# An attention and two feed-forward layers on one core: the order of the engines' work within a pair of tiles, and in the last steps, written anew

## What is computed

```python
h = shift_token(x)                      # second half of the columns moved down by one row
q, k, v = split(h @ wqkv)               # 8 heads of 64
q, k = rotary_xpos(l2norm(q) * qs, l2norm(k) * ks)
o = local_attention(q, k, v)            # windows of 128: each row sees its own and the previous window
x = x + o @ wo
h = layernorm(shift_token(x)) * g + b
a, g = split(h @ w1 + b1)               # 2 x 682 columns
x = x + (a * gelu(g)) @ w2 + b2
```

## Time and profile before

| | |
|---|---|
| median of three runs | 2774.15 us (2766.67 to 2779.47) |
| the profiled execution | 2765.1 us |
| its span, first to last instruction | 2762.9 us |
| granted TensorE clock, mean | 0.983 |
| instructions | 65920 |
| second phase | from about 291 us to the end |

### The profile page before, as it was taken

How to read it: one execution, slowest core, us unless ns; L and a number is a source line. 1 busy time by engine, 2 the same in 40 slices (tenths; PEclk the granted TensorE clock), 3 DMA queues, 4 the chain that set the end, 5 groups by cost and what they waited for, 6 DMA issues and landing times.

```text
span 2762.9 us, 65920 instructions
## 1 busy us (share of the span) xinstructions
PE 2674.0 (97%) x22240; PEld 2347.6 (85%) x22240; DVE 2257.7 (82%) x7122; ACT 1889.5 (68%) x4798; POOL 1649.6 (60%) x1753
## 2 busy tenths in 40 slices
PE   8998699999999999999999999999999999999996
PEld 5776478888888888888988888888888888888886
DVE  5776578888888888888887888888888888988884
ACT  5565367767777777777776777767777767777773
POOL 3444456666656566655555666676666666666662
PEclk9999799999999999999999999999999999999998
DMA  5566210000000000000002311110111110011110
GB/s 181 182 198 196 101 44 28 24 28 25 24 26 28 26 26 28 21 26 28 26 26 81 107 35 32 36 36 27 32 35 32 36 35 29 30 35 32 36 30 22
DMA packets 144511, 140.39 MB, mean 51 GB/s; under 512 B 16024, under 2 KB 126128, under 8 KB 143408
## 3 DMA queue, kind: packets, MB, share of 16 engines
q1 hardware_dynamic: 144176, 136.18, 15.6%
HBM read 80.02 MB, written 51.92 MB: 48 GB/s over the span
## 4 chain that ended last, share of the span: by engine, by line
PE 83%; DVE 2%; DMA 1%; ACT 1%; issue 1%; SPq 1%; POOL 0%; DVEq 0%; POOLq 0%; ACTq 0%
PE p_wide L95 13%; PE p_wide L97 12%; PE p_wide L96 12%; PE p_values L1680 9%; PE p_turn L1668 8%; PE p_mixed L95 5%; PE p_mixed L97 5%; PE p_mixed L96 5%; PE p_score L95 4%; PE p_turn L1635 2%; PE p_score L96 2%; PE p_score L97 2%; PE p_turn L1642 2%; PE p_mixed L1600 1%; PE p_mixed L1698 1%
## 5 line engine op out<-in xcount | busy, mean ns | idle before, releaser
L1114 POOL TENSOR_TENSOR prob<-prob,rinv 128x512 f32<-128x512 f32 (+1 forms) x512 | 498.4, 989 | 504.6 <-DVE rinv L1402 504.2
L1217 ACT ACTIVATE prob<-prob,least 128x256 f32<-128x256 f32 (+1 forms) x1024 | 498.5, 488 | 68.4 <-DVE least L1394 65.4
L1394 DVE CUSTOM_DVE_ANT_0 prob<-p_score,mask,inv_norm 128x256 f32<-128x256 f32 (+1 forms) x1024 | 442.1, 459 | 53.3 <-issue 50.0
L1092 POOL TENSOR_TENSOR inv_norm<-norm_clipped,minus_half 128x8 f32<-128x8 f32 x256 | 439.0, 1715 | 74.2 <-DVE norm_clipped L1360 67.4
L1226 ACT ACTIVATE pT<-p_turn 128x512 f32<-128x512 f32 (+1 forms) x512 | 270.4, 566 | 245.5 <-PE p_turn L1668 243.8
L95 PE MATMUL p_wide<-hT_h,w_h 128*128 128x256 f32 (+1 forms) x1408 | 414.1, 294 | 5.3 <-DVE hT_l L1450 4.2
L97 PE MATMUL p_wide<-hT_h,w_l 128*128 128x256 f32 (+1 forms) x1408 | 396.5, 282 | 0.0
L96 PE MATMUL p_wide<-hT_l,w_h 128*128 128x256 f32 (+1 forms) x1408 | 395.8, 281 | 0.0
L95 PE MATMUL p_wide<-wqkv_h,xT_h 128*128 128x512 f32 x768 | 330.0, 430 | 6.2 <-DVE rope_sin L1344 4.0
L1248 ACT ACTIVATE gelu<-p_wide,columns 128x256 f32<-128x256 f32 x320 | 151.7, 474 | 228.5 <-PE p_wide L97 226.9
L97 PE MATMUL p_wide<-wqkv_h,xT_l 128*128 128x512 f32 x768 | 307.2, 400 | 0.0
(11 more groups left out here) (134 smaller groups left out, 7620.7 us busy)
## 6 DMA issues: line engine op xcount, KB each, us to landing
x_tile<-x_rows SPq DMA_DIRECT2D x192, 128.0 KB, 2.1
a_wraw<-in_w_all SPq DMA_DIRECT2D x32, 264.0 KB, 4.4
w_high<-a_wraw_h SPq DMA_DIRECT2D x32, 264.0 KB, 2.4
w_low<-a_wraw_l SPq DMA_DIRECT2D x32, 264.0 KB, 3.0
a_x<-in_x SPq DMA_DIRECT2D x32, 256.0 KB, 4.7
x_rows<-a_x SPq DMA_DIRECT2D x64, 128.0 KB, 1.8
x_tile<-x_rows SPq DMA_DIRECT2D x128, 64.0 KB, 2.0
mid_rows<-x_mid SPq DMA_DIRECT2D x128, 64.0 KB, 1.5
```

Source lines behind the costliest of these rows:

```text
L1092: pool.tensor_tensor(r[:, t.slot(2), heads], rt[:, heads], half[:, heads], ALU.pow).then_inc(pool_r[n], 1)
L1114: pool.tensor_tensor(p, p, rinv[:, 2 * m:2 * m + 2].unsqueeze(2).to_broadcast([P, 2, cols.stop - cols.start]), ALU.mult).then_inc(pool_p, 1)
L1217: act.activation(prob[:, h, cols], prob[:, h, cols], ACT.Exp, bias=least[:, h:h + 1], scale=-1.0, accum_out=rsum[:, h:h + 1]).then_inc(act ...
L1394: dve.tensor_tensor_reduce(prob[:, h, cols], p_score[h % 2][:, c0 + cols.start:c0 + cols.stop], mask[:, a.slot(2), cols], r[:, a.slot(2), ...
```

## The change

```diff
@@ PE, first part of step @@
             def step(st_):
                 T, Q = st_.tile, st_.pair
                 T, Q = st_.tile, st_.pair
+                if T(6):
+                    after((act_pT, T(6), 4, 2))
+                    after((pool_p, T(6), 4, 4))
+                turn_probs(T(6), 3)
+                if T(4):
+                    after((dve_kr, T(4), 1, 1))
+                project_v(T(4))
                 if T(5):
-                    vacant((act_pT, T(6), 4, 4), (act_pT, T(6), 4, 2), (dve_kT, T(5), 1, 1), (act_pT, T(7), 4, 4), (dve_kT, T(6), 1, 1), (act_pT, T(7), 4, 2))
-                turn_probs(T(5), 1)
+                    after((act_pT, T(6), 4, 3))
+                    after((pool_p, T(5), 4, 1))
+                turn_probs(T(5), 0)
+                if T(3):
+                    after((dve_x, T(9), 1, 1), (dve_xT, T(4), 1, 1))
+                    if not T(9):
+                        after((dve_xT, T(4), 1, 1))
+                turn_x(T(3))
+                scores(T(5), 1)
+                values(T(6), 0)
+                values(T(6), 1)
...
@@ PE, end of step @@
+                if T(3):
+                    if not T(4):
+                        after((dve_qT, T(3), 1, 1))
+                scores(T(3), 0)
+                if T(2):
+                    after((dve_gt, Q(4), HF + 1, 6), (dve_xT, T(2), 1, 1))
+                project_k(T(2), 0)
+                project_k(T(2), 1)
+                if T(8):
+                    after((dve_gT, Q(4), HF + 1, 6), (dve_xT, T(2), 1, 1))
+                narrow(T(8))
...
@@ DVE, least_of and middle @@
                         need(dve, pe_pT, a.done(4, 2 * group - 2))
-                        at = 2 * a.slot(2) + group
-                        dve.memset(took[:, at:at + 1], 0.0)
...
-                    need(dve, pool_res, c.done(1, -1))
+                    if c.g < LAYER + 2:
+                        need(dve, pool_res, c.done(1, -1))
+                    else:
+                        dve.wait_ge(pool_r1, c.done(1, -1 - LAYER))
...
@@ SP, step, the new order @@
+                refill("q", T(2))
+                store_mid(T(6))
+                load_shifted(T(6))
+                load_x1(T(8))
+                store_mid(T(5))
+                load_shifted(T(5))
+                refill_tables(T(2), 0)
+                refill("w2", T(8))
+                load_x(T(1))
+                refill_tables(T(2), 1)
+                refill("w1", T(6))
                 refill("wo", T(4))
+                load_x1(T(7))
+                store_x(T(8))
+                store_x(T(7))
+                refill("k", T(0))
+                load_x(T(0))
                 refill("v", T(0))
...
@@ ACT, step, the new order from widen's results to the exponentials @@
                 gelu(Q(4), 3)
+                q_high(T(3))
+                gated_high(Q(4), 2)
+                gated_high(Q(4), 3)
+                x_high(T(2))
+                gelu(Q(4), 4)
+                gelu(Q(4), 5)
                 probs_out(T(4), 0)
                 gated_high(Q(4), 4)
                 gated_high(Q(4), 5)
+                exponential(T(4), 4)
...
@@ DVE, step, the new order of its last third @@
+                gated(Q(4), 2)
+                gated(Q(4), 3)
+                least_of(T(4), 7)
                 q_low(T(3))
                 gated_low(Q(4), 2)
+                x_low(T(2))
                 gated(Q(4), 4)
+                gated(Q(4), 5)
                 gated_low(Q(4), 3)
                 gated_low(Q(4), 4)
                 gated_low(Q(4), 5)
+                statistics(T(5))
                 least_of(T(3), 0)
+                normed(T(6))
                 least_of(T(3), 1)
+                normed(T(5))
+                least_of(T(3), 2)
                 inverse_sums(T(4), 1)
+                x_new(T(8))
```

More of the change, by code:

```diff
@@ L782, in slot, with back, __init__ @@
     def slot(self, ring):
[L783 removed]
+        return self.g % ring
     def uses(self, ring, more=0):
[L787 to L790 removed]
+        return self.g // ring + more
+    def back(self, n):
+        return Tile(self.g - n)
 class Pair:
[L796 to L798 removed]
+    def __init__(self, first):
+        self.first, self.second, self.layer = first, first.back(-1), first.layer
@@ L800, in done, with __init__ @@
     def done(self, per, more=0):
[L802 to L807, removed]
+        return per * (self.first.g // 2) + more
 class Step:
-    def __init__(self, i, w, layer=None):
-        self.i, self.w, self.layer = i, w, layer
+    def __init__(self, n):
+        self.n = n
     def tile(self, lag):
[L818 to L822, removed]
+        g = 2 * self.n - lag
+        return Tile(g) if 0 <= g < TILES else None
@@ L824, in pair, with all_steps @@
     def pair(self, lag):
         first = self.tile(2 * lag)
[L827 to L837, removed]
+        return Pair(first) if first else None
+def all_steps(step, first, end):
+    for n in range(first, end):
+        step(Step(n))
 def layers_phase(nc, x_d, mid_d, wh_d, wl_d, tab_d, out, shared):
@@ L1072, in _ @@
+            all_steps(step, 0, 60)
+            last_steps()
             for n in range(2):
@@ L1580, in _, with after @@
+            all_steps(step, 0, 60)
+            last_steps()
         @block.tensor
         def _(pe):
-            def vacant(*readers):
-                for semaphore, last_reader, per, more in readers:
-                    if last_reader:
-                        pe.wait_ge(semaphore, last_reader.done(per, more))
+            def after(*done):
+                for semaphore, tile, per, more in done:
+                    if tile:
+                        pe.wait_ge(semaphore, tile.done(per, more))
@@ L1787, in step @@
-                widen(Q(4), 3)
+                    if not T(5):
+                        after((dve_q, T(3), 1, 1))
+                    if not T(5):
+                        after((act_pT, T(5), 4, 3))
+                turn_q(T(3))
+                if Q(4):
+                    after((dve_gt, Q(4), HF + 1, 3), (dve_qr, T(3), 1, 1))
+                widen(Q(4), 4)
+                if T(2):
+                    if not T(8):
+                        after((dve_mid, T(5), 1, 1), (dve_xT, T(3), 1, 1))
+                    if not T(5):
+                        after((dve_xT, T(3), 1, 1))
@@ L1802, in step @@
-                turn_probs(T(4), 1)
-                scores(T(3), 0)
-                values(T(4), 0)
-                project_q(T(2))
-                if T(2):
-                    vacant((dve_gt, Q(4), HF + 1, 6), (dve_gt, Q(4), HF + 1, 4), (dve_gt, Q(4), HF + 1, 2), (act_v, T(3), 1, 1), (dve_kr, T(3), 1, 1), (act_v, T(4), 1, 1))
+                if T(4):
+                    after((pool_p, T(4), 4, 2))
+                turn_probs(T(4), 1)
+                if T(3):
+                    if not T(4):
+                        after((dve_qT, T(3), 1, 1))
```

2116 lines of the change are left out of this document (1917 added, 199 removed).

## The result

The changed kernel takes **2734.67 us** (median of four runs, 2732.14 to 2740.91) against 2773.81 (four runs of the kernel before); the ratio is 0.9875, 95% interval 0.9853 to 0.9896. Two later sets gave 2737.14 (0.9878) and 2737.19 (0.9874). The forecast was 2733.

What follows compares the result with a forecast made beforehand. PE's stream was taken as the bound. Switches -30, last steps -12, border -2 and new waits +3 sum to -41 us; the 9 us difference to the median applied, the forecast is 2733 us, range 2700 to 2756.

Steps and rivals of the forecast that it cites:

- What bounds the kernel: Steady pairs: PE waits for nothing, so its stream's sum sets the 37.5 us a pair.
- The prediction's signs: Signs of being right: four pairs in about 147.6 us, values in two runs of 32, no recurring PE waits.
- Price of a switch, 0.59 us a pair: Steady pairs: 14 switches become 10, saving 0.59 us a pair, 33.6 us over 57 pairs.
- the rival that switches are worth nothing: The price lies in the change of stationary load kind; only the tail gain stays: 2760 us, chance 0.08.
- Cover and new waits, +3: At narrow(T8) and the like, the last gT_l is only 0.2 to 0.35 us early; 0 to 10 us charged, 3 taken.
- the mechanism of the rival: Narrow(T8) comes before its last gT_l and PE stops in every pair; ScalarE late gives 2797 us; chance 0.08.
- DVE did not take over in layer one: Rival in layer one: DVE's strict order eats that layer's whole saving: 2748 us, chance 0.14.
- Memsets, 0: 256 memsets of 0.059 us leave DVE, 0.24 us a pair; DVE is not the bound, so nothing on the path.
- Border, -2: At the layers' border, the late x tile queues behind the k weights alone: -2 us, within 2 either way.
- The last steps, -12: At the end, 22 us of waits and low clock become about 10: -12 us, bounds 4 and 18.
- under 9: Sign of being right: the tail's PE gaps sum to under 9 us.
- +3.5: The 22 extra switches of the end, at 0.16 us each, give back 3.5 us.

Runs made afterwards that it cites:

- experiment 5: Kernel before, with values(T4, 0) and values(T4, 1) moved into the next step's group, 14 to 11 switches a pair: 2767.85 us, ratio 0.9991.
- Experiment 8: Changed kernel without its written-out end (the step runs to the end, two waits added), run twice: 2727.86 and 2727.70 us, ratios 0.9856 and 0.9838.
- experiment 7: Changed kernel with scores(T4, 1) moved ahead of widen(Q4, 0), straight behind the values, 10 to nine switches a pair: 2730.81 us, ratio 0.9854.
- experiment 3: Changed kernel with widen(Q4, 0) and turn_probs(T5, 0) each moved between values, four switches more a step: 2812.79 us, ratio 1.0149.

## Why the prediction was right, and where not

- **What bounds the kernel:** right. In the steady pairs PE's waits are too few and short to count in either kernel; the pair became shorter by what the stream lost. Splitting and merging move the time with PE's switches, in the new and in the old order. The prediction's signs came true here: 147.8 us for four pairs (147.6 forecast), and the values in two runs of 32.
- **Price of a switch, 0.59 us a pair:** 0.55 measured in layer zero (14.8 us over 28 pairs, 0.53). Splits and merges moved the pair by 0.13 to 0.17 us a switch wherever no wait was in the way, and the rival that switches are worth nothing falls. The estimate from the Trainium skill (TensorE: Matmul & The Clock Gate, Single matmul latency), 0.166 for any kind, would give 0.66 us a pair for four; the measurement is below it, and below the sum by kinds too. That a change of tiling mode drains the engine, as the Trainium skill has it (TensorEngine Tiling (Array Packing), Key Properties), agrees with these runs; none of them separates the draining from another cost of the same change.
- **Cover and new waits, +3:** right in kind and nearly in size. Layer one gains 12.0/26 = 0.46 us a pair instead of layer zero's 0.53. Narrow is held up only in some pairs, mostly by less than the profile prints as idle: beyond the shortest such step, its starts in the 54 steady pairs take 5.4 to 6.4 us in three profiles, before 0.8. So the term was about 5 and not 3, within its 0 to 10. The slack of a few tenths was real: experiment 5 uses it up and pays. So was the mechanism of the rival; that ScalarE comes late by a table load was not met in the change. DVE did not take over in layer one.
- **Memsets, 0:** right for the change; its removal gave nothing, and seems to have cost 0.06 us a pair.
- **Border, -2:** 2.0 to 3.8 less.
- **The last steps, -12: this step failed.** I took pauses and half clock as 22 us that would become 10. Over the last eight pairs they were 24.9 and became 18.0 to 21.4. The waits that the new order shortens were costed rightly: from narrow(120) on, PE's idle time is 8.5 us, and "under 9" was the forecast's sign. What it makes in the five pairs ahead was put at nothing: 4.8 us of idle time, and most of the 4.2 us of short waits. The extra switches cost 1.8 us where 3.5 was forecast. For the section called "end" above, the forecast was +3.5 and -12, together -8.5; measured is +0.9, +1.8 and +4.1. Experiment 8 isolates it: without the written-out end, that section takes 283.9 and 287.8 us, 3 to 7 less than before and 4 to 11 less than in the change. (Against before, each of these figures holds the 1.8 us of moved work.)
- **Why the total was right all the same: luck in part.** From profile to profile the forecast was 2765.1 - 41 = 2724, and the profiled execution after took 2735.9: 12 us too little gain. Of these, 9.4 are the last steps; the pairs fall 3.8 short (26.8 for 30.6), and the border gives 1.6 more than its 2. The medians gained 39, 32 and 37 us in three sets, because the kernel before usually runs at a lower clock than in its profile (mean 0.9797 in 42 runs, 0.983 in the profile), and the changed kernel's mean is 0.9841. Over all runs the means of the two kernels are 35 us apart: 22.2 of it is full-clock time, the rest clock. The forecast held no such term: two errors of opposite sign met, and the median's 2734.67 beside the forecast's 2733 is by chance closer than the sum was. Part of the clock's share is the end (18.0 us at half clock before; 4.8, 7.9 and 12.3 after); where the rest comes from isn't settled, since the first 400 us vary from run to run (58 to 75 us at half clock in three profiles of the same kernel).

## What to carry to other kernels

When PE is busy all the time, count the changes between stationary shapes in its order and price each kind from start-to-start times; removing one pays its price only while buffers and the other engines' orders still fit, so look for the slack of the tightest wait first and move the other engines along. Run the plain steady order to the end before writing an end by hand, and measure the hand-written one against that, not against the old kernel. Compare executions by time multiplied by mean granted clock when a few us decide.

## What the runs showed of the hardware that I had not expected

- A switch's price depends on its kind and is small: 0.14 and 0.155 us around a lone group of values, 0.20 to 0.23 out of scores or values into a wide product, 0.23 values into scores (experiment 7); an averaged 0.14 in experiment 3.
- Within one kernel, time varies with the mean granted clock and hardly with anything else (standard deviation of the product 0.6 to 3.5 us).
- A memset of 59 ns on VectorE, off the path, goes with a shorter pair: 28 pairs 1032.7 us with it and 1035.6 without; in the kernel with nine switches 1030.3 and 1032.2. About a third of it in the first of these programs (1.0 of 2.9 us) lies where narrow starts. I have no cause for it; it was seen in both programs and nothing was run to explain it.
